# Conv attention, linear attention and mixture of experts in one kernel: two-part router product, unscaled queries, and another order of work

## What is computed

```python
h = group_norm(x, gn_scale, gn_bias)
q, k, v = nin(h, Wq, bq), nin(h, Wk, bk), nin(h, Wv, bv)
w = softmax(einsum(q, k) * C ** -0.5)          # 1024 x 1024 scores per image
x = x + nin(einsum(w, v), Wp, bp)
t = to_tokens(x)                               # [b, 1024, 128]
t = t + linear_attention(ln(t)) @ W_out + b_out  # 4 heads, keys' softmax over the tokens
n = ln(t)
logits = n @ router_w.T                        # 8 experts, the best two with their shares
out = n + sum_e combine[:, e] * (gelu(n @ w1[e] + b1[e]) @ w2[e] + b2[e])
x = from_tokens(t + out)
```

## Time and profile before

| | |
|---|---|
| median of 3 runs | 333.72 us (333.65 to 334.03) |
| the profiled execution | 334.79 us |
| its span, first to last instruction | 332.9 us |
| busy: PE, DVE, ACT, POOL | 301.8, 256.0, 191.8, 102.1 us |

### The profile page before, as it was taken

The page is one execution under the profiler, slowest core; times in us unless marked ns, Lnnn a source line. Parts: engine busy times, 40 slices in busy tenths (PEclk is TensorE's granted clock), DMA queues, the critical chain, the costliest instruction groups (busy, mean ns, idle before and its releaser), DMA issues.

```text
span 332.9 us, 5172 instructions
## 1 busy us (share of the span) xinstructions
PE 301.8 (91%) x1569; PEld 235.6 (71%) x1569; DVE 256.0 (77%) x623; ACT 191.8 (58%) x332; POOL 102.1 (31%) x154
## 2 busy tenths in 40 slices
PE   2887989989989899789989996999999997999995
PEld 2776868777968677577768785867757774666884
DVE  4799686678686798987687885787688685777995
ACT  3356474676570586445277656458567435856883
POOL 2345350059102664500636200089120037000000
PEclk9999999999999999999999999999999999999999
DMA  5902000010000011000000106396520692239511
GB/s 152 300 0 66 0 1 2 0 66 0 0 3 0 0 65 64 2 12 0 0 1 0 63 12 201 132 376 255 172 91 0 177 372 112 71 116 385 189 33 63
DMA packets 12757, 29.58 MB, mean 89 GB/s; under 512 B 2192, under 2 KB 5952, under 8 KB 10816
## 3 DMA queue, kind: packets, MB, share of 16 engines
q1 hardware_dynamic: 12448, 29.00, 25.3%
q10 hardware_dynamic: 288, 0.33, 0.3%
HBM read 24.73 MB, written 4.59 MB: 88 GB/s over the span
## 4 chain that ended last, share of the span: by engine, by line
PE 59%; DVE 23%; issue 7%; ACT 4%; DMA 3%; POOL 2%; SPq 1%; DVEq 0%; POOLq 0%; ACTq 0%
PE ring L1403 7%; PE ring L1721 6%; PE ring L1405 6%; PE ring L1404 6%; PE ring L1418 6%; PE scores L1403 6%; PE scores L1405 6%; PE scores L1404 6%; DVE prob L1019 4%; DVE pT_lo L1026 4%; PE ring L1555 2%; DVE lst L1056 2%; ACT prob L674 2%; PE ring L1533 2%; DVE t L1045 1%
## 5 line engine op out<-in xcount | busy, mean ns | idle before, releaser
L819 ACT ACTIVATE gel<-scores,b_c 128x512 f32<-128x512 f32 x64 | 43.9, 688 | 35.6 <-PE scores L1405 32.5
L1019 DVE TENSOR_SCALAR_CACHE_REDUCE prob<-scores 128x1024 f32<-128x1024 f32 x32 | 38.9, 1215 | 12.1 <-PE scores L1405 12.0
L1026 DVE TENSOR_TENSOR pT_lo<-ring,pT_hi 128x512 fp32r<-128x512 f32 x64 | 40.7, 681 | 8.1 <-ACT pT_hi L680 7.6
L556 POOL TENSOR_SCALAR rstd<-lmv 128x8 f32<-128x8 f32 x8 | 2.1, 260 | 135.3 <-DVE lmv L1062 135.3
L680 ACT ACTIVATE pT_hi<-ring 128x512 fp32r<-128x512 f32 x64 | 34.3, 598 | 14.5 <-PE ring L1418 14.5
L674 ACT ACTIVATE prob<-prob,row_max 128x1024 f32<-128x1024 f32 x32 | 36.8, 1151 | 9.5 <-DVE prob L1019 9.3
L1418 PE MATMUL ring<-ident,prob 128*128 128x128 f32 x256 | 33.9, 276 | 8.2 <-ACT prob L674 5.8
L1418 PEld LDWEIGHTS ring<-ident,prob 128*128 128x128 f32 x256 | 28.4, 140 | 14.0 <-ACT prob L674 6.1
L1403 PE MATMUL scores<-wT_hi,w_hi 128*128 128x512 f32 x64 | 34.2, 534 | 0.0
L1403 PE MATMUL scores<-k_both,q_hi 128*128 128x512 f32 x64 | 27.3, 427 | 0.9 <-DVE k_both L1004 0.9
L1403 PE MATMUL ring<-pT_hi,v_hi 128*128 128x512 f32 x64 | 26.7, 417 | 1.2 <-DVE pT_lo L1026 1.2
(11 more groups left out here) (297 smaller groups left out, 725.9 us busy)
## 6 DMA issues: line engine op xcount, KB each, us to landing
pT_hi<-scratch_s SPq DMA_DIRECT2D x8, 1024.0 KB, 6.6
prob<-scratch_s SPq DMA_DIRECT2D x4, 1024.0 KB, 7.7
k_both<-scratch_s SPq DMA_DIRECT2D x3, 1024.0 KB, 6.7
z_in<-scratch_z SPq DMA_DIRECT2D x8, 256.0 KB, 3.2
out_dram<-out_s SPq DMA_DIRECT2D x8, 256.0 KB, 2.2
xb<-in_x_dram SPq DMA_DIRECT2D x3, 512.0 KB, 3.1
scratch_z<-out_s SPq DMA_DIRECT2D x2, 512.0 KB, 2.8
k_both<-scratch_s SPq DMA_DIRECT2D x4, 256.0 KB, 4.4
```

The lines of the kernel that those rows point to most:

```text
L819: act.activation(half(gel, s % 2), scores[:, s % 2, :], ACT.Gelu, bias=b1_c[:, s % E:s % E + 1]).then_inc(e_gelu, 1)
L1019: dve.tensor_scalar(prob[:, i % 2, :], scores[:, 2 * (i % 2):2 * (i % 2) + 2, :].rearrange("p a t -> p (a t)"), -1.0, None, ALU.mult, ALU. ...
L1026: dve.tensor_tensor(tile_group(pT_lo, n, i), as_tiles(ps(place, unit)), tile_group(pT_hi, n, i).bitcast(FP32), ALU.subtract).then_inc(drai ...
```

## The change

Seven things, all in one edit:

1. The router's parts stand side by side: `router_two` has the high part in columns 0 to 7 and the low part in 8 to 15, `router_top` the high part in 0 to 7. `logits` makes two products per half (wT_hi by router_two, wT_lo by router_top) where it made three. The 16 rows are copied and transposed, and DVE adds the two groups of 8 with one more reduction, into `logit`.
2. Queries are no longer scaled; `row_maximum` multiplies by -SCALE instead of -1. The `p1T` copies of the weights go, and the low parts come from one scalar_tensor_tensor each; `bqs_c` goes.
3. `h_f` of image 0 is made by GpSimd, once; both DVE computations go.
4. In the opening q0's first two products wait for wq_hi alone, `first_biases` stands behind q0, `keep_busy` makes four products instead of six.
5. Another order in the turns: `turn_o` ahead of `gather_keys` and the residual add ahead of `take_g` with units g and OT0 in each other's bank; the last softmax ahead of the copies of T6; the residual add of the old image ahead of maximum 1; the low part of q1 behind the o adds; scores 3, 4, 5 earlier on PE; maximum 4 behind the low parts of T3; `key_sums` ahead of `route_c`.
6. `hidden` of steps 0 and 1 stands ahead of T7's transposes and behind `merge2`.
7. `WHOLE` has 24 steps instead of 33 (out: 2, 3, 5, 11, 14, 23, 28, 29, 39); some positions in `TAIL_AT`, `END_AT` and `POOL_AT` differ by a step or more.

The diff, cut to what is spoken of:

```diff
-                    PV0=1, T4a=2, T4b=3, T5a=0, T5b=1, p0=2, p1=3, g=0, OT0=1)
+                    PV0=1, T4a=2, T4b=3, T5a=0, T5b=1, p0=2, p1=3, OT0=0, g=1)
...
-                  T4b=1, T5a=2, T5b=3, p0=0, p1=1, c0=2, c1=3, g=0, OT0=1)
+                  T4b=1, T5a=2, T5b=3, p0=0, p1=1, c0=2, c1=3, OT0=0, g=1)
...
-TAIL_AT = dict(m3=0, PV=0, o=0, st=2, OT=5, OTst=5, w0=9, w1=11, lg=12, u0=12, u1=14, lT=16, rA=17, kT=20, exp=20, rB=20, ks=23, z=17, p=21, rC=20, g=23, c=24)
-END_AT = dict(ctx=25, m2=27, m3=28, o=29, st=29, w0=34, w1=35, lg=36, lT=38, rA=38, exp=38, rB=38, rC=39, z=41, c=41)
+TAIL_AT = dict(m3=0, PV=0, o=0, st=2, OT=5, OTst=5, w0=9, w1=11, lg=12, u0=14, u1=14, lT=16, rA=17, kT=20, exp=20, rB=20, ks=23, z=17, p=21, rC=20, g=23, c=23)
+END_AT = dict(ctx=24, m2=27, m3=28, o=29, st=29, w0=35, w1=36, lg=37, lT=38, rA=38, exp=38, rB=38, rC=39, z=41, c=41)
...
-POOL_AT = dict(n2=0, n1=9, nr=9, ab=18, n2e=30, nre=38)
-
-
-WHOLE = frozenset((2, 3, 4, 5, 6, 7, 11, 12, 14, 15, 16, 17, 18, 19, 22, 23, 24, 26, 27, 28, 29, 31, 32, 33,
-                   34, 37, 38, 39, 40, 42, 43, 44, 45))
+POOL_AT = dict(n2=0, n1=6, nr=12, ab=18, n2e=30, nre=38)
+
+
+WHOLE = frozenset((4, 6, 7, 12, 15, 16, 17, 18, 19, 22, 24, 26, 27, 31, 32, 33, 34, 37, 38, 40, 42, 43, 44,
+                   45))
...
+            pool.wait_ge(ld_x0b, 16)
+            pool.tensor_scalar(h_f[:, :], xb[:, :], gmul[:, 0:1], gadd[:, 0:1], ALU.mult, ALU.add).then_inc(h_f_made, 1)
...
                 softmax(b, 6)
+                softmax(b, 7)
                 turn_probs(after_place, 6)
-                softmax(b, 7)
...
-                dve.tensor_scalar(wq_sc, wq_raw, SCALE, g, ALU.mult, ALU.mult)
-                dve.tensor_scalar(wq_hi[:, :], wq_raw, SCALE, g, ALU.mult, ALU.mult)
+                dve.tensor_scalar(wq_hi[:, :], wq_raw, g, None, ALU.mult).then_inc(setup_made, 1)
                 after(dve.tensor_tensor(gadd[:, 0:1], gsum[:, 0, 0:1], g, ALU.mult))
                 dve.tensor_scalar(gadd[:, 0:1], gadd[:, 0:1], -1.0, gb_c, ALU.mult, ALU.add).then_inc(gn_made, 1)
-                dve.tensor_tensor(wq_lo[:, :], wq_sc, wq_hi[:, :].bitcast(FP32), ALU.subtract).then_inc(setup_made, 1)
+                dve.wait_ge(setup_made, 1)
+                scaled_low(wq_raw, g, wq_hi[:, :], wq_lo[:, :]).then_inc(setup_made, 1)
                 dve.wait_ge(ld_w["wk"], 16)
-                dve.tensor_scalar(wk_sc, wk_raw, g, None, ALU.mult)
                 after(dve.tensor_scalar(wk_hi[:, :], wk_raw, g, None, ALU.mult))
-                dve.tensor_tensor(wk_lo[:, :], wk_sc, wk_hi[:, :].bitcast(FP32), ALU.subtract).then_inc(setup_made, 1)
-                dve.wait_ge(bqs_made, 1)
+                scaled_low(wk_raw, g, wk_hi[:, :], wk_lo[:, :]).then_inc(setup_made, 1)
...
                 wait_filled(dve, SETUP, "bias_qk")
-                both = ps(SETUP, "bias_qk")
-                dve.tensor_scalar(bias_first[:, 0:1], both[:, 0:1], SCALE, bqs_c, ALU.mult, ALU.add)
-                after(dve.tensor_tensor(bias_first[:, 1:2], both[:, 1:2], bk_c, ALU.add))
+                after(dve.tensor_tensor(bias_first[:, 0:2], ps(SETUP, "bias_qk")[:, 0:2], cols[:, 0:2], ALU.add))
...
-            first_norm()
...
-                after(dve.tensor_copy(rt_hi[:, 0:E], ps(FIRST, "rowsT")[:, 0:E]))
-                dve.tensor_tensor(rt_lo[:, 0:E], ps(FIRST, "rowsT")[:, 0:E], rt_hi[:, 0:E].bitcast(FP32),
-                                  ALU.subtract).then_inc(drained[FIRST.bank("rowsT")], 1)
+                dve.tensor_copy(router_top[:, 0:E], ps(FIRST, "rowsT")[:, 0:E])
+                after(dve.tensor_copy(router_two[:, 0:E], ps(FIRST, "rowsT")[:, 0:E]))
+                dve.tensor_tensor(router_two[:, E:2 * E], ps(FIRST, "rowsT")[:, 0:E],
+                                  router_two[:, 0:E].bitcast(FP32), ALU.subtract).then_inc(drained[FIRST.bank("rowsT")], 1)
...
-                                  -1.0, None, ALU.mult, ALU.min, accum_out=row_max[:, i:i + 1]).then_inc(s_max, 1)
+                                  -SCALE, None, ALU.mult, ALU.min, accum_out=row_max[:, i:i + 1]).then_inc(s_max, 1)
...
-                    logits = ps(place, "lT")[:, 0:TILES * E].rearrange("p (j e) -> p j e", e=E)
-                    link("routing", lc, red(top, logits, AX.X, ALU.max, negate=True))
-                    tt(less, logits, over(top), ALU.add).then_inc(drained[place.bank("lT")], 1)
+                    parts = ps(place, "lT")[:, 0:2 * TILES * E].rearrange("p (j k e) -> p j e k", k=2, e=E)
+                    link("routing", lc, red(logit[:, :, :], parts, AX.X, ALU.add))
+                    link("routing", lc, red(top, logit[:, :, :], AX.X, ALU.max, negate=True))
+                    tt(less, logit[:, :, :], over(top), ALU.add).then_inc(drained[place.bank("lT")], 1)
...
-                project(place, b, "q1", q_hi, q_lo, bqs_c)
                 take(place, "wvT", wvT[:, :])
-                first_norm()
                 group_stats(1)
                 row_maximum(place, b, 0)
                 merge_weights()
+                project(place, b, "q1", q_hi, q_lo, bq_c)
...
-                row_maximum(place, b, 4)
                 group_deviation(place, 1, B - 1)
                 turn_probs(place, b, 3)
+                row_maximum(place, b, 4)
...
-                project(place, b, "q1", q_hi, q_lo, bqs_c)
                 invert_sums(la, 1)
                 if lc is not None:
                     take_out(place, lc, 0)
                     take_out(place, lc, 1)
+                project(place, b, "q1", q_hi, q_lo, bq_c)
+                if lc is not None:
...
                 row_maximum(place, b, 0)
+                residual(place, la, 1)
                 row_maximum(place, b, 1)
-                residual(place, la, 1)
...
                 turn_probs(place, b, 2)
+                turn_probs(place, b, 3)
                 row_maximum(place, b, 4)
-                turn_probs(place, b, 3)
...
+                key_sums(place, la)
+                if lc is not None:
                     route_c()
-                key_sums(place, la)
...
-                take_g(place)
                 dve.wait_ge(t1b_made, la + 1)
                 residual(place, b, 0)
+                take_g(place)
...
-            keep_busy(6)
+            keep_busy(4)
...
+                pe.wait_ge(h_lo_made, b * HALVES + n + 1)
+                if unit == "q0" and place is FIRST:
+                    dst, x_hi = open_unit(place, unit), half(h_hi, n)
+                    pe.wait_ge(setup_made, 1)
+                    pe.matmul(dst, hi[:, :], x_hi, start=True, stop=False)
+                    pe.matmul(dst, hi[:, :], half(h_lo, n), start=False, stop=False)
+                    pe.wait_ge(setup_made, 2)
+                    fill(place, unit, pe.matmul(dst, lo[:, :], x_hi, start=False, stop=True))
+                    return
...
-                    whole(place, f"lg{n}", (rt_hi[:, :], rt_lo[:, :]), w_of(lb, n))
+                    dst, (w_hi, w_lo) = open_unit(place, f"lg{n}"), w_of(lb, n)
+                    pe.matmul(dst, router_two[:, :], w_hi, start=True, stop=False)
+                    fill(place, f"lg{n}", pe.matmul(dst, router_top[:, :], w_lo, start=False, stop=True))
...
+                first_biases()
...
+                for unit in ("q0", "k0"):
                     wait_drained(pe, place, unit)
-                score(b, 0)
+                score(b, 0, lambda: wait_drained(pe, place, "k1"))
...
+                score(b, 3)
                 turn_probs(place, b, 1)
                 turn_x(place, b)
-                score(b, 3)
+                wait_drained(pe, place, "q1")
+                score(b, 4)
...
                 turn_probs(place, b, 2)
-                wait_drained(pe, place, "q1")
-                score(b, 4)
                 if lc is not None:
                     logits(place, lc)
+                score(b, 5)
                 turn_probs(place, b, 3)
-                score(b, 5)
...
+                turn_o(place, 0)
                 gather_keys(place)
-                turn_o(place, 0)
...
-                    hidden(m, s)
+                    if not (first_batch(m) and s < 2):
+                        hidden(m, s)
...
+            pe.wait_ge(experts_split, 3)
+            pe.wait_ge(mask_made, 1)
+            hidden(0, 0)
             turn_probs(TAIL, la, 7)
             merge2(TAIL)
-            pe.wait_ge(experts_split, 3)
-            pe.wait_ge(mask_made, 1)
+            hidden(0, 1)
...
```

65 lines of the change are left out of this document (29 added, 36 removed).

## The result

The changed kernel takes 331.56 us (median of 5 runs, 330.52 to 332.18) against 333.72 us of the kernel before (333.49 to 335.22, 5 runs): ratio 0.9908, 95% interval 0.9885 to 0.9930. That is 3.1 us faster by the ratio, 2.2 us by the medians. The forecast was 325.2 us and its range ended at 330.5. The sign was right, and the gain a quarter (by the medians) to a third (by the ratio) of what was forecast. A second measurement of the same kernel gave 331.38 us, ratio 0.9912 [0.9888, 0.9937].

What follows compares the result with a forecast made beforehand. PE and DVE wait for each other in the attention turns; PE bounds the expert part. Terms 1.4 + 1.3 + 1.8 + 0.6 + 0.7 + 0.9 + 1.2 + 0.6 = 8.5 us off 333.72 give 325.2 us, range 322.0 to 330.5.

Steps and rivals of the forecast that it cites:

- Plain steps: Expert part: nine more steps split, each saving PE 0.18 us; 1.2 us faster, bounds 0 and 1.6.
- The summed logits: Loop's turns: one added DVE reduction, 0.22 us, about 0.26 with its wait, counted inside the 0.9 us gain a turn.
- Opening: Start of kernel: second score maximum 1.4 us earlier, at about 19.3 us; bounds 0 and 1.65.
- The clock: Rival, opening: with two fillers fewer PE's full clock may come later than 13.8 us; 327.6 us, chance 0.12.
- The turns: Attention turns: 1.3 us gained at turn ends, 1.8 inside the loop's two turns, 0.6 at the first turn's key maximum.
- The hoisted products: Expert part: two expert products fill PE's wait for T7 and the shares, saving one product, 0.7 us.
- The logits: Expert part: four logit products fewer in two batches, 0.23 us each, 0.9 us faster.
- w0 one step later: Near the end: one expert step done before PE's 1.87 us wait for w_n; 0.6 us faster, bounds 0 and 1.4.
- The first rival: Whole kernel: only removed work pays, places in the queues give nothing; 4.4 us faster, 329.3 us, chance 0.22.

Runs made afterwards that it cites:

- e1: The changed kernel with the 33 plain expert steps of before put back: 328.04 us, ratio 0.9826 of before.
- b1: The kernel before with only the plain steps changed, 24 instead of 33: 339.65 us, ratio 1.0183 of before.
- e7: The changed kernel with the summed logits written to spare columns of their PSUM bank instead of an SBUF tile: 328.59 us, ratio 0.9834 of before.
- e8: The changed kernel with only steps 2, 3, 5, 11 and 14 plain again: 327.80 us, ratio 0.9800 of before.
- e4: The changed kernel with six filler products ahead of q0 instead of four: 330.23 us, ratio 0.9905 of before.
- d1: The changed kernel measured and profiled a second time, unaltered: 331.38 us, ratio 0.9912 of before; span 326.5 us.
- e6: The changed kernel with the first two expert products back behind the second part of the context: 331.92 us, ratio 0.9937 of before.
- e5: The changed kernel with TAIL_AT, END_AT and POOL_AT put back to before, its 24 plain steps kept: 334.00 us, ratio 0.9992 of before.
- c1: The changed kernel with the edits of e8 and e7 together: 326.45 us, ratio 0.9777 of before.
- c3: c1 with steps 28 and 29 plain as well: 326.22 us, ratio 0.9759 of before; measured again 326.58 us, 0.9757.
- e9: The changed kernel with only steps 23, 28, 29 and 39 plain again: 329.38 us, ratio 0.9854 of before.
- the c kernels: c1, c3, c1 with e3's edit added, and c3 with DVE's copy of m ahead of the first share's product: ratios 0.9777, 0.9759, 0.9809, 0.9719 of before.
- e2: The changed kernel with the turned logits' bank given back by the first reduction instead of the add behind it: 331.19 us, ratio 0.9904 of before.
- e3: The changed kernel with tile 4's score maximum ahead of T3's low parts again, in the turns: 329.44 us, ratio 0.9869 of before.

## Why the prediction was wrong

Point by point, by its own terms:

- **Plain steps (1.2 forecast): the step that failed.** The prediction: each split step "adds 0.68 us to DVE and 0.62 to ACT", and "where DVE is full of routing some of it comes back", 1.2 with the bounds 0 and 1.6. The product's saving of 0.18 stands in its rows; what failed is the overlap: the bounds took the work on DVE as free or as eating up the saving, and left out a loss. I looked for cover in DVE's sum over the expert part (98.1 of 129.3 us); five of the nine steps stand where GpSimd makes w_n and u, on which PE waits next. There DVE's denser queue holds GpSimd (w_n 6.39 us instead of 3.94, the pair 19.0 instead of 15.2), and PE pays where u comes late. Measured: 2.7 us lost (e1), 6.1 in the kernel before (b1), so the term was wrong by 3.9 us.
- **The summed logits (counted as 0.22 us of DVE per turn).** The prediction had the hold by GpSimd in its rows and applied it to the key minimum and to h_f, but not to the add whose operand the change moves from PSUM to SBUF. So it had the cost of the add wrong: 2.21 us instead of 0.22, ten times, in each of the two turns of the loop. Its price for the kernel is 2.5 us (e7), and the traces place it in the second turn.
- **Opening (1.4): right** at an equal clock (e8, 19.29). In after's profile the later change of the clock took 0.7 of it back. The clock was a rival, but I tied it to the two fillers, and e4 shows no effect of them.
- **The turns (1.3, 1.8 and 0.6, with the opening 5.1 by the start of the last linear output): about right.** 4.3 were measured with the held add in both turns (5.8 in d1, where the clock rose early), and 6.8 without it (e7: 207.79 to 200.98). That the total came out near the 5.1 is in part luck: it contains a loss of some 2 us by the held add that no term had, so the terms themselves were too low. In all of these kernels the two hoisted products stand ahead of the last linear output; their gain is not in these figures.
- **The hoisted products (0.7): not refuted** (e6, 1.0 against after, with an interval of 0.1 to 1.9).
- **The logits (0.9)** were not tried by themselves.
- **w0 one step later (0.6): not as priced.** PE's wait for w_n fell only from 1.87 to 1.68, and with the low parts of 28 and 29 gone to 0.47. The lists as a whole are worth 2.8 us (e5), but against a loss that the same change brings.

The two misses make 3.9 + 2.5 = 6.4 us, and 8.5 - 6.4 = 2.1 is near the 2.2 to 3.1 measured. The sum is rough, and its closeness is luck in part, since the two cures overlap by 1.7 us (c1); less by this, the misses make 4.7 and leave 3.8. A better test: without the term of the plain steps the forecast is 7.3 us, and with seven of the nine steps plain and the logits in PSUM the rest of the change gives 8.1 us by the ratio (c3).

The first rival's time (329.3) came nearest, but its mechanism is not what happened: the places in the queues did pay. What was missing is a rival in which the expert part loses time, by split steps that hold the engine on which PE waits next.

Open: why PE waits about 1 us (0.81 to 1.28) for the DMA of the combination rows (308.01 in after) in the edits of the changed kernel that have the five steps and step 39 split, and not in e1, e8, e9 and the c kernels; b1, with both split, has no such wait. Also open is how the expert steps' gain divides between e8's five and e9's four, since together they give no more than the five alone.

## What to carry to other kernels

Before work is moved to an engine "with room", find the stretch in which it lands and ask who waits for whom there; a sum over a part of the kernel hides it. On this chip ask of every DVE and GpSimd operation where its operands lie: a small copy from PSUM to SBUF can turn a 0.2 us operation into one of 2 us while the other engine runs. And take a wait of PE away by curing what is late: removing only the dependency (e2) left the engine behind it as late and saved nothing.

## What the runs showed of the hardware that was not expected

- The hold acts both ways: DVE held by GpSimd (0.22 to 2.21 us for an add of 64 elements), and GpSimd by DVE (w_n 3.91 to 6.39 us for the same 8 instructions, a single one 0.45 to 1.47).
- PE's clock, at 1.2 GHz where products start 0.43 us apart and at 2.4 GHz where they start 0.23 apart: in one and the same kernel it rose at 16.3 us in one execution and at about 11.0 in another. Behind waits of 2.45, 2.60, 2.79 and 3.63 us (b1, e5) the products ran at the lower level for some 3 us, and behind one of 1.81 (e3, at 202.74) as well; behind those of 1.75 and 1.87 us (after at 231.52, before at 277.38) they did not.
- Two profiles of one kernel (after and d1) differ by 3.3 us in span, more than the whole measured effect. A difference of waits between two single traces is not yet the effect of the change.
